# Ninth slot for gathered key and value rows; own rows and x1 loaded ahead of the MLP weights

## What is computed

```python
x = layernorm(x + self_attention(x, W_qkv, b_qkv))      # 16 heads of 32, rope on q and k
# cross attention over a tree: K, V = projections of ctx; parents are pairwise means (K) and sums (V)
flatK, flatV = concat(levels of K), concat(levels of V)  # 1023 rows for each batch
nk, nv = flatK[:, :, idx_table], flatV[:, :, idx_table]  # 12 rows for each token
logits = concat([Q . K, Q . nk]); w = softmax(logits)    # 13 logits for each head
o = w . concat([V, nv])
x = layernorm(x + o @ Wo.T + bo)
x = layernorm(x + relu(x @ w1 + b1) @ w2 + b2)           # MLP, width 2048
```

## Time and profile before

| what | value |
|---|---|
| device time, median of 3 executions | 2299.0 us (2291.67 to 2299.38) |
| the profiled execution: device time, and its span | 2284.85 us, 2283.0 us |
| granted TensorE clock, mean over the span | 0.952 |
| busy: PE, DVE, ACT, POOL | 87%, 81%, 46%, 49% of the span |
| line 1696, indirect gathers | 384 issues, 972 ns each on POOL |
| bytes moved by the gathers' queue | 201.35 MB of 392.51 MB |

### The profile page before, as it was taken

The page is one execution under the profiler, slowest core; times in us unless marked ns, Lnnn a source line. Parts: engine busy times, 40 slices in busy tenths (PEclk is TensorE's granted clock), DMA queues, the critical chain, the costliest instruction groups (busy, mean ns, idle before and its releaser), DMA issues.

```text
span 2283.0 us, 34454 instructions
## 1 busy us (share of the span) xinstructions
PE 1982.2 (87%) x11744; PEld 1042.2 (46%) x11744; DVE 1852.2 (81%) x2416; ACT 1057.4 (46%) x1854; POOL 1127.2 (49%) x1132
## 2 busy tenths in 40 slices
PE   5699999999999999877249998999899899989997
PEld 2244444344444444322025555555555555555655
DVE  7579888889898898878688888888888888888940
ACT  3255555555555555544114444444444444444443
POOL 3325555545364555362554554645645546546520
PEclk9799999999999999989579999999999999999999
DMA  5344343435444443434855756656667567566520
GB/s 185 112 125 130 121 141 117 155 123 158 130 130 157 128 134 128 146 126 150 298 189 208 247 187 230 225 201 239 207 209 257 186 212 242 193 238 226 194 75 19
DMA packets 188809, 392.51 MB, mean 172 GB/s; under 512 B 20692, under 2 KB 82260, under 8 KB 188632
## 3 DMA queue, kind: packets, MB, share of 16 engines
q1 hardware_dynamic: 133336, 188.91, 25.6%
q0 software_dynamic: 55296, 201.35, 25.4%
HBM read 312.33 MB, written 77.59 MB: 171 GB/s over the span
## 4 chain that ended last, share of the span: by engine, by line
DVE 28%; PE 12%; DMA 7%; POOL 6%; issue 5%; SPq 2%; ACT 1%; DVEq 0%; POOLq 0%; ACTq 0%
DVE e_ps L1501 7%; DVE swapped L1448 5%; DMA inputs<-kv_flat,idx_rows 5%; DVE inputs L1439 5%; DVE inputs L1497 4%; PE aux L900 3%; POOL inputs L1696 3%; POOL inputs L1724 2%; PE misc_ps L924 2%; PE o_ps L924 2%; PE rows_ps L860 1%; PE e_ps L860 1%; POOL tree L1622 1%; SPq L575 1%; DMA nodes<-kv_flat 1%
## 5 line engine op out<-in xcount | busy, mean ns | idle before, releaser
L1696 POOL DMA_INDIRECT inputs<-kv_flat,idx_rows x384 | 373.4, 972 | 136.2 <-issue 91.4
L1375 DVE TENSOR_REDUCE neg_max<-rows_ps 128x1 f32<-128x512 f32 x512 | 326.7, 680 | 88.7 <-PE rows_ps L784 85.6
L729 PE MATMUL aux<-inputs 128*128 128x512 f16 x1536 | 358.3, 386 | 32.1 <-POOL inputs L1607 21.5
L900 PE MATMUL aux<-probs,queries 128*128 128x256 f16 x2048 | 357.4, 277 | 0.7 <-issue 0.7
L1724 POOL TENSOR_TENSOR inputs<-inputs,split_up 128x1024 f32<-128x1024 f32 x96 | 182.6, 1916 | 245.0 <-DVE split_up L1485 244.3
L1501 DVE TENSOR_TENSOR e_ps<-e_ps,inputs 128x512 f32<-128x512 f32 x384 | 268.3, 699 | 42.6 <-POOL inputs L1724 20.8
L1102 ACT ACTIVATE probs<-e_ps 128x1024 f32<-128x1024 f32 x256 | 261.9, 1023 | 77.3 <-PE e_ps L816 75.1
L900 PE MATMUL aux<-probs,keys 128*128 128x256 f16 x1024 | 282.5, 276 | 0.0
L729 PEld LDWEIGHTS aux<-inputs 128*128 128x128 f16 x1536 | 151.0, 99 | 218.4 <-POOL inputs L1607 21.5
L1416 DVE TENSOR_TENSOR probs<-probs 128x2048 f32<-128x2048 f32 x96 | 230.4, 2400 | 16.8 <-ACT probs L1102 16.7
L1448 DVE TENSOR_REDUCE swapped<-inputs 128x32 f32<-128x1024 f32 x192 | 229.7, 1212 | 0.0
(11 more groups left out here) (164 smaller groups left out, 3427.3 us busy)
## 6 DMA issues: line engine op xcount, KB each, us to landing
kv_flat<-nodes SPq DMA_DIRECT2D x128, 256.0 KB
nodes<-kv_flat SPq DMA_DIRECT2D x32, 512.0 KB
queries<-qk_dram SPq DMA_DIRECT2D x96, 128.0 KB, 2.7
keys<-qk_dram SPq DMA_DIRECT2D x96, 128.0 KB, 3.0
split_up<-in_pieces SPq DMA_DIRECT2D x40, 256.0 KB
inputs<-in_xT SPq DMA_DIRECT2D x8, 1024.0 KB, 6.3
inputs<-in_ctxT SPq DMA_DIRECT2D x8, 1024.0 KB, 7.6
qk_dram<-high SPq DMA_DIRECT2D x32, 256.0 KB, 2.2
```

What stands on the lines that cost most here:

```text
L729: mm = pe.matmul(o[:], w_part[:, w, c, f], x_part[:, which, c, :], start=c + k == 0, stop=c == KC - 1 and k == 2)
L900: mm = pe.matmul(HB[c % 2][:, 0:RW], w[:, k, c * P:(c + 1) * P], x_part[:, k, half * RW:(half + 1) * RW], start=k + i == 0, stop=k == KC - ...
L1375: dve.tensor_reduce(neg_max[:, g % 2, at + i:at + i + 1], rows_ps[:, i, :], AX.X, ALU.max, negate=True).then_inc(max_done, 1)
L1696: pool.indirect_dma_start(nb[:, slot(lt, g), k, :], None, rows, bass.IndirectOffsetOnAxis(idx_rows[:, lt, at:at + 1], 0))\
```

## The change

Nine slots take the place of eight. Slots 0 to 7 stay in `inputs`; the ninth lies in the last third of `probs`, where the transposed MLP input (`x2T_hi`, `x2T_lo`) was. That input moves onto the memory of `xb` (now called `res`), the residual rows of the first stage. A slot's number now counts through all batches, since 24 groups are not a multiple of 9. POOL's first gather into the ninth slot waits for the end of the softmax in `probs`, and ACT's first write of x2T waits until POOL has split the last x1 out of `xb`. On SP's queue the x1 loads of tiles 2 and 3 and the own row of tile 1 move from step 18 to step 15, ahead of the four weight loads.

```diff
-SLOTS = 8
+SLOTS = 9
...
-            nb, = over(inputs, (F32, P, SLOTS, GN, 2 * D))
+            nb, = over(inputs, (F32, P, SLOTS - 1, GN, 2 * D))
...
-            w2_lo, x2T_hi, x2T_lo = over(probs, (F16, P, WC, D), (F16, P, KC, T), (F16, P, KC, T))
+            w2_lo, last_slot = over(probs, (F16, P, WC, D), (F32, P, GN, 2 * D))
+            res = sb("res", [P, 4 * 1024], F16)
+            xb, = over(res, (F32, P, TT, D))
+            x2T_hi, x2T_lo = over(res, (F16, P, KC, T), (F16, P, KC, T))
...
-            xb = sb("xb", [P, TT, D])
...
-            def slot(lt, g):
-
-                return (lt * NG + g) % SLOTS
+            def slot(b, lt, g):
+
+                return ((b * TT + lt) * NG + g) % SLOTS
 
             def fills(b, lt, g):
 
-                return b * (TT * NG // SLOTS) + (lt * NG + g) // SLOTS + 1
+                return ((b * TT + lt) * NG + g) // SLOTS + 1
+
+            def rows_in(b, lt, g):
+
+                at = slot(b, lt, g)
+                return nb[:, at] if at < SLOTS - 1 else last_slot
...
                         load_res(0, 0)
+                        load_x1(0, 2)
+                        load_x1(0, 3)
+                        load_own(0, 1)
                         for dst, part in zip(w1_sb, parts):
...
-                    if d == 18:
-                        load_own(0, 1)
-                        load_x1(0, 2)
-                        load_x1(0, 3)
...
                 x2_apply(0, 0)
+                act.wait_ge(x1_lo_done, START + B * TT)
                 turned_x2(0, 0)
...
-                    if GATHER_CROSS < d <= GATHER_CROSS + SLOTS:
+                    if GATHER_CROSS < d < GATHER_CROSS + SLOTS:
                         gather(0, d - GATHER_CROSS - 1)
...
                     if d == 15:
-                        for i in range(NG + AHEAD, NG + AHEAD + 4):
+                        pool.wait_ge(misc_ready, START + misc_number(B, "share", 14, False, True) + 1)
+                        for i in range(NG + AHEAD - 1, NG + AHEAD + 3):
                             gather(0, i)
                     if d == 18:
-                        for i in range(NG + AHEAD + 4, 2 * NG + AHEAD):
+                        for i in range(NG + AHEAD + 3, 2 * NG + AHEAD):
                             gather(0, i)
```

More of the change, by code:

```diff
@@ L1436, in multiply @@
                         if g < NG:
-                            dve.wait_ge(gathered[slot(lt, g)], (16 * GN) * fills(b, lt, g))
-                            kk = nb[:, slot(lt, g), :, 0:D]
+                            dve.wait_ge(gathered[slot(b, lt, g)], (16 * GN) * fills(b, lt, g))
+                            kk = rows_in(b, lt, g)[:, :, 0:D]
                             dve.tensor_tensor(kk, kk, q.unsqueeze(1).to_broadcast([P, GN, D]), ALU.mult)\
@@ L1448, in reduce @@
                             dve.tensor_reduce(logits[:, lt % 2, g * GN:(g + 1) * GN, :],
-                                              nb[:, slot(lt, g), :, 0:D].rearrange("p n (h d) -> p n h d", h=H),
+                                              rows_in(b, lt, g)[:, :, 0:D].rearrange("p n (h d) -> p n h d", h=H),
                                               AX.X, ALU.add).then_inc(k_sum, 1)
@@ L1493, in multiply @@
                     def multiply(g):
-                        dve.wait_ge(gathered[slot(lt, g)], (16 * GN) * fills(b, lt, g))
-                        vv = nb[:, slot(lt, g), :, D:2 * D].rearrange("p n (h d) -> p n h d", h=H)
+                        dve.wait_ge(gathered[slot(b, lt, g)], (16 * GN) * fills(b, lt, g))
+                        vv = rows_in(b, lt, g)[:, :, D:2 * D].rearrange("p n (h d) -> p n h d", h=H)
                         w = w_ps[:, g * GN:(g + 1) * GN, :].unsqueeze(3).to_broadcast([P, GN, H, DH])
@@ L1500, in accumulate @@
                         dve.wait_ge(o_part, START + n * O_STEPS + 1 + g * GN + k)
-                        dve.tensor_tensor(ROW[:], ROW[:], nb[:, slot(lt, g), k, D:2 * D], ALU.add).then_inc(o_part, 1)
+                        dve.tensor_tensor(ROW[:], ROW[:], rows_in(b, lt, g)[:, k, D:2 * D], ALU.add).then_inc(o_part, 1)
                     multiply(0)
@@ L1695, in gather @@
                         at = g * GN + k
-                        pool.indirect_dma_start(nb[:, slot(lt, g), k, :], None, rows,
+                        pool.indirect_dma_start(rows_in(b, lt, g)[:, k, :], None, rows,
                                                 bass.IndirectOffsetOnAxis(idx_rows[:, lt, at:at + 1], 0))\
-                            .then_inc(gathered[slot(lt, g)], 16)
+                            .then_inc(gathered[slot(b, lt, g)], 16)
                 def summed(b, i):
@@ L1720, in weight_values @@
                     for g in groups:
-                        pool.wait_ge(gathered[slot(lt, g)], (16 * GN) * fills(b, lt, g))
-                        vv = nb[:, slot(lt, g), :, D:2 * D].rearrange("p n (h d) -> p n h d", h=H)
+                        pool.wait_ge(gathered[slot(b, lt, g)], (16 * GN) * fills(b, lt, g))
+                        vv = rows_in(b, lt, g)[:, :, D:2 * D].rearrange("p n (h d) -> p n h d", h=H)
                         w = weights[:, g * GN:(g + 1) * GN, :].unsqueeze(3).to_broadcast([P, GN, H, DH])
```

## The result

| what | before | after |
|---|---|---|
| device time, median of 4 executions each | 2295.34 us (2289.20 to 2299.38) | 2231.59 us (2224.24 to 2236.46) |
| ratio | | 0.9728, 95% interval 0.9702 to 0.9753 |
| the profiled execution: device time, and its span | 2284.85 us, 2283.0 us | 2224.24 us, 2222.4 us |
| granted TensorE clock, mean over the span | 0.952 | 0.959 |
| a round, from tile 4's turn to tile 30's, divided by 13 | 69.66 us | 64.96 us |

The change is faster by 2.7%, 64 us between the medians. In the changed kernel the lines stand 6 or 7 further down: the key product L1439 is L1446, the sum L1501 is L1508, the turn L841 is L847, the query's product L860 is L866.

The account below looks back on a forecast made before the run. The prediction took a loop through several engines, with late gathers delaying DVE and idling PE, as the bound. Rounds 56 + outside tiles 8 + start 2 = 66 us off 2299 gave 2233 us, range 2220 to 2245.

Parts of the forecast that it names:

- Rounds: Second stage, two tiles each: 69.7 us become 65.4, 4.3 us less in each of 13, 56 us in all.
- Leg B: Second tile's turn to the next first tile's: gathers land sooner, 34.5 us become 31.5.
- Leg A: First tile's turn to second tile's: set by PE's way to the next query, 13.4 + 19.8 + 0.7 = 33.9 us.
- The clock: PE in the rounds: idle shrinks to about 1.4 us a round, so the falls to 0.50 should go.
- What is late next: DVE in each round: it waits for the next query, 1 to 2 us.
- Tiles 2, 4 and 31: Tiles outside the 13 rounds: each gains 3.2 - 0.45 us of gather waits, 8 us together.
- The start: Start of the second stage: own row issued about 1088.7, x1 store lands about 1134 for 1136.3, 2 us won.
- Gathers stay late: Rival, POOL's gathers: issued earlier into a full queue they land little sooner, 2283 us, chance 0.08.
- the slot doesn't move the path: Rival, leg B: something hidden behind the gathers holds it, only the start gains, 2297 us, chance 0.07.
- The clock still falls: Rival, PE in leg A: clock falls once a round, query after 15.2 us, round 67.2, 2257 us, chance 0.12.
- Slower: Rival, SP's queue at the start: slow weights make the x1 store and tile 2's query late, 2319 us, chance 0.04.
- Better: Rival, start and rounds: start wins 9 us more, rounds reach PE's own 64, 2206 us, chance 0.07.

Follow-up runs that it names:

- e5: The changed kernel run a second time, unaltered, on another chip: 2235.21 us, ratio 0.9724.
- e9: The changed kernel run a third time, unaltered: 2232.86 us, ratio 0.9702.
- e2: The changed kernel with SP's queue in its old order, tile 1's own row and the x1 loads behind the weights: 2238.46 us, ratio 0.9780.
- e10: The same kernel as e2, nine slots with SP's old order, run again on another chip: 2230.17 us, ratio 0.9710.
- e11: The same kernel as e4, w2 loads behind the store of x1, run again beside the changed kernel: 2216.71 us, ratio 0.9659.
- e6: The changed kernel with the query of two tiles on issued one piece of the MLP sooner in PE's program: 2245.69 us, ratio 0.9775.
- e8: The changed kernel with the edits of e4 and e6 together, later w2 loads and sooner query: 2238.64 us, ratio 0.9746.
- e12: The changed kernel with POOL's product of group 5 one gather group later: 2305.29 us, ratio 1.0038.
- e4: The changed kernel with the two w2 loads moved behind the store of x1 on SP's queue: 2223.83 us, ratio 0.9730.
- e1: The changed kernel with eight slots in place of nine, all else of the change kept: 2287.80 us, ratio 0.9996.
- e3: The kernel before the change, PE's idle ahead of each first tile's turn filled with 12 thrown-away matmuls: 2284.61 us, ratio 0.9986.
- e7: The changed kernel with POOL's product of group 5 one gather group sooner: 2362.37 us, ratio 1.0261.
- first two sets: The runs e1 to e4 and e5 to e8, each set on one chip with runs of the kernel before.
- third set: The runs e9 to e12, on one chip with runs of the kernel before.

## Why the prediction was right

The forecast was 2233 us, 66 us less than before. Measured are 2231.59 us and 64 us less, inside its own range of 2220 to 2245. By its steps, in the first profile of the change:

- **Rounds, 56 us.** Measured (69.66 - 64.96) x 13 = 61 us. The profile of before is one with "remote" waits of ACT, though; with e5 as its like the gain is (69.66 - 65.61) x 13 = 53 us, and no profile of before with prompt signals exists. The forecast round of 65.4 lies between 64.96 and 65.61.
- **Leg B, 31.5 us.** Measured 31.79. The wait for gathers was put at 0.45 us a tile between 0.2 and 1.2, and is 0.45 (0.58 in e5, 0.66 in e9), nearly all of it at group 5, with groups 3 and 4 in time, as the forecast had it. POOL's issues stayed and each carries the next group, and the place in the burst decides when a group lands: what stood in the third place was there 1656.44 - 1642.34 = 14.1 us after the burst's first issue before, and what stands there now lands 14.3 us after it (median of 28 bursts in the first profile of the change).
- **Leg A, 33.9 us.** Measured 33.17. The 0.7 us to the turn hold. DVE's part is 19.3 and 19.8 us in turn from round to round, so 19.8, read from one round, was 0.25 too much in the mean. From turn to query 12.8 us, not 13.4. The 13.4 came from a profile in which ACT starts late: at full clock it is 13.4 to 13.6 us in nearly all rounds of e2 to e5, whose signals are late (e5 has a leg A of 33.79), and 12.8 in nearly all of the first profile, e9, e10 and e11, whose signals are prompt. No row of the trace of before shows 12.8.
- **The clock.** Its falls go, one is left. PE's idle of 1.5 us in most rounds answers to the 1.4 forecast. But the forecast leaned on one row, the 2.58 us that had lowered nothing, and that was no safe mark: in the same trace 2.16 us ahead of tile 24's turn came with a fall, and so did 1.9 to 2.0 us in e6, e8 and e12. The Trainium skill (TensorE: Matmul & The Clock Gate, "What's actually happening") says that the gate's window runs free of the program; the trace of the change agrees in that idle of 2.92 us ahead of tile 16's turn lowered nothing and idle of 2.94 us ahead of tile 24's did.
- **What is late next.** The query, as said: 23.9 us in 14 rounds, 1.7 a round, forecast 1 to 2.
- **Tiles 2, 4 and 31, 8 us.** From the end of tile 1's sum to tile 31's 1039.2 became 972.3 us; less the rounds' 61 that leaves 6 us.
- **The start, 2 us.** The own row was issued at 1095.49, 6.8 us of first stage taken off 1088.7, the very time forecast. The store landed at 1142.77 - 6.8 = 1136.0, as before, where 1134 was forecast: from 1095 to 1143 us the queues moved 16.79 MB at 350 GB/s, 6% below the 373 that I had used. From sum to sum 61.9 us for 62.8, so 0.9 us. The reading that the wait for the own row would turn into one for tile 2's query holds (it is 16.67 us, where the two were 11.56 and 8.46 us before), and e4 and e11 confirm the cause: with the store ahead of w2 ACT waited 7.47 us for it, not 16.07.

```profile
DMA packets 10689, 16.79 MB, mean 350 GB/s; under 512 B 320, under 2 KB 8512, under 8 KB 10688
```

- **The rivals.** "Gathers stay late" and "the slot doesn't move the path" fall by the 0.45 us and by e1. "The clock still falls" falls by the trace; its price, forecast at 67.2 - 65.4 = 1.8 us a round, shows in the one round with a fall, whose query ends 14.5 us after the turn and not 12.8. At eight slots it was 0.6 by e3, hidden by late rows. "Slower" needed a store landing far past 1136; it landed at 1136. "Better" assumed rounds down to PE's own 64 and 9 us at the start: the start is to be had (e11), the rounds aren't, at least not by moving the query (e6) or POOL's product (e7, e12).
- The sum was right in part because errors cancelled: leg A gained 0.7 us a round more than forecast (9 us in all, in the first profile), leg B 0.3 us a round less (4 us), the three tiles 2 us and the start 1 us less.

## What to carry to other kernels

Total an engine's waits by cause, but price a removed wait in the loop of one round: here 93.5 us of waits gave 53 to 61 us in the rounds, because half of them stood in leg A, beside a query that would have been late anyway. Where two limits stand side by side, one removed alone shows next to nothing (e3 took one and won 0.6 us of 2.4). Before an instruction moves earlier on its engine, look at what it covers: in a chain that crosses two engines and back, the piece in between is the cover, and a wait left bare can cost the clock as well (e6). And on a loading queue, what the next step stores goes ahead of weights that are not due for long: one moved pair of loads gave 7.6 and 9.4 us.

## What the runs showed of the hardware

**Signals can be late while POOL issues gathers.** All profiles of the first two sets, and the one of the kernel before, lack the record of many semaphore updates and have engines starting late behind what released them: ACT up to 2.5 us in before, 5.2 in e5 and 6.2 in e7, where 0.04 us is usual. In e5, of 2756 updates by PE, ACT, DVE and POOL from 1270 to 2110 us, 582 have no record at the end of their instruction, and 573 of these fall between the first issue of a burst of gathers and 1.5 us past its last, which is 56% of the time. In the first profile of the change and all four of the third set not one of some 2780 is missing (2591 in e12). The lateness goes with the set, so perhaps with the chip, and costs 0.4 to 0.7 us a round: 65.61 us in e5 for 64.96 and 65.22, 65.64 in e2 for 65.02 in e10, 65.64 in e4 for 64.93 in e11. What makes it the runs don't show, nor whether measuring has a part in it: span and granted clock were taken in every execution.

**The clock can fall around an idle of 2 us.** PE's idle of 1.9 to 2.0 us came with a granted clock of 0.50 for 3.4 us in four rounds of e6, while waits as long ahead of the same line in other rounds of e6 did not; 3.1 us ahead of tile 28's turn in e1 didn't either. The length of an idle alone does not decide it.

**The same program starts its second stage 13 us sooner or later** (1062 to 1075 us) with no edit in the first: five executions can't tell 4 us, a profile from sum to sum can.

**A load of 2 MB in rows of 1 KB holds SP's queue for 10 to 12 us** when 4 and 6 MB are ahead of it in the queue (11.77 and 10.76 us for the two w2 loads of the change), and for 0.5 and 2.9 us when none or 2 MB are (e11). In the old order (e2) the same two loads held it for 6.0 and 15.6 us. What is issued behind waits as long: the two small stores of x1 took 15.09 us.
